# Scores of two key tiles in one stretch, value products in one stretch, turned probabilities in place

## The reference

```
x = x + cross_attention(layernorm(x), ctx)            # 16 sequences of 256 rows, 256 channels
y = layernorm(x)
for layer in range(2):                                # on y
    q, k, v = split(shift_token(y) @ wqkv)            # 8 heads of 64
    q, k = l2norm(q)*qs, l2norm(k)*ks; rotary_xpos(q, k)
    o = local_attention(q, k, v)                      # windows of 128 rows, each sees itself and the one before
    y = y + o @ wo
    h = layernorm(shift_token(y)) * lg + lb
    a, g = split(h @ w1 + b1)
    y = y + (a * gelu(g)) @ w2 + b2
x = x + y
```

## Time and profile before

| | |
|---|---|
| median of 3 runs | 1419.7 us (1419.18 to 1420.46) |
| profiled execution, span | 1416.2 us |
| what lies around the span (median less span) | 3.5 us |
| TensorE busy | 1385.3 us (98%) |
| VectorE, ScalarE, GpSimd busy | 77%, 66%, 54% |
| chain that ended last | TensorE 65%, VectorE 16%, ScalarE 9% |

### The profile page before, as it was taken

One profiled execution on the slowest core, in us unless ns is written; L12 is line 12 of the kernel. 1 busy time (PEld: TensorE's weight loads), 2 busy tenths in 40 slices (PEclk: granted clock), 3 DMA queues, 4 the chain that ended last, 5 costly groups with the idle time before them and its releaser, 6 DMA issues.

```text
span 1416.2 us, 32735 instructions
## 1 busy us (share of the span) xinstructions
PE 1385.3 (98%) x11563; PEld 1237.8 (87%) x11563; DVE 1090.6 (77%) x3067; ACT 935.8 (66%) x2662; POOL 761.9 (54%) x576
## 2 busy tenths in 40 slices
PE   8999999989999999999999999999999999999998
PEld 7999998778888888888888888888888888888887
DVE  5777776768788788888888878778778888888874
ACT  6877777456666666666666667666666666666662
POOL 1212222556566566666666667666656666666653
PEclk9999999999999999999999999999999999999999
DMA  5223122101100100010001211111111111111001
GB/s 190 90 92 110 48 67 90 47 20 29 30 30 30 30 29 28 28 28 28 28 29 29 71 29 37 33 35 37 37 37 37 36 36 36 36 36 37 29 30 31
DMA packets 50516, 63.41 MB, mean 45 GB/s; under 512 B 8402, under 2 KB 32104, under 8 KB 50408
## 3 DMA queue, kind: packets, MB, share of 16 engines
q1 hardware_dynamic: 50408, 61.99, 14.0%
HBM read 38.17 MB, written 16.78 MB: 39 GB/s over the span
## 4 chain that ended last, share of the span: by engine, by line
PE 65%; DVE 16%; ACT 9%; issue 5%; DMA 2%; POOL 1%; SPq 1%; DVEq 0%; ACTq 0%; POOLq 0%
PE pb L567 30%; PE pb L880 6%; PE pb L894 6%; PE pb L856 5%; PE pb L825 5%; PE pb L840 5%; ACT x_p L1079 4%; PE pb L920 4%; DVE p_t L1596 2%; DVE p_t L1610 2%; ACT x_pt L1085 2%; DVE r_sin L1583 2%; DVE n_sq L1562 2%; DMA x<-x 1%; DVE r_cos L1577 1%
## 5 line engine op out<-in xcount | busy, mean ns | idle before, releaser
L1823 POOL TENSOR_TENSOR n_inv<-n_cl,half_neg 128x16 f32<-128x16 f32 x64 | 211.2, 3299 | 178.2 <-DVE n_cl L1567 174.7
L1222 ACT ACTIVATE p_t<-p_t,s_nm 128x128 f32<-128x128 f32 (+1 forms) x512 | 227.0, 447 | 22.3 <-DVE s_nm L1596 20.9
L567 PE MATMUL pb<-h_hi,w_hi 128*128 128x256 f32 x704 | 207.5, 295 | 1.3 <-DVE h_lo L1558 1.2
L567 PE MATMUL pb<-h_hi,w_lo 128*128 128x256 f32 x704 | 198.7, 282 | 0.0
L567 PE MATMUL pb<-h_lo,w_hi 128*128 128x256 f32 x704 | 198.6, 282 | 0.0
L1828 POOL TENSOR_TENSOR r_cos<-r_cos,r_sin 128x1024 f32<-128x1024 f32 x64 | 154.6, 2415 | 53.8 <-DVE r_sin L1583 53.8
L1213 ACT ACTIVATE pt_t<-pb 128x512 f32<-128x512 f32 x192 | 114.3, 597 | 98.5 <-PE pb L840 97.8
L1178 ACT ACTIVATE qk_sq<-pb 128x512 f32<-128x512 f32 x128 | 72.5, 592 | 142.9 <-PE pb L567 141.5
L567 PE MATMUL pb<-wqkv_hi,xt_hi 128*128 128x512 f32 x384 | 163.9, 427 | 2.6 <-DVE r_sin L1583 2.3
L1859 POOL TENSOR_TENSOR hg_lo<-hg,hg_hi 128x256 fp32r<-128x256 f32 (+1 forms) x192 | 141.9, 760 | 44.5 <-DVE hg_hi L1627 44.5
L1596 DVE CUSTOM_DVE_ANT_0 p_t<-pb,mask_t 128x128 f32<-128x128 f32 (+1 forms) x512 | 151.9, 353 | 17.5 <-PE pb L825 17.3
(11 more groups left out here) (145 smaller groups left out, 3907.5 us busy)
## 6 DMA issues: line engine op xcount, KB each, us to landing
y_state<-x SPq DMA_DIRECT2D x32, 256.0 KB, 2.0
x_cur<-y_state SPq DMA_DIRECT2D x32, 256.0 KB, 2.6
x_res<-y_state SPq DMA_DIRECT2D x32, 256.0 KB, 2.8
x_in<-x SPq DMA_DIRECT2D x16, 256.0 KB, 2.9
x_state<-x SPq DMA_DIRECT2D x16, 256.0 KB, 2.0
x_orig<-x_state SPq DMA_DIRECT2D x16, 256.0 KB, 2.9
out<-x SPq DMA_DIRECT2D x16, 256.0 KB, 2.2
x<-x SPq DMA_DIRECT2D x32, 112.0 KB, 2.3
```

The source lines that it names most:

```text
L567: mm = pe.matmul(dst, s, m, start=(n == 0 and k == 0), stop=(n == len(pairs) - 1 and k == 2))
L1222: e = nc.scalar.activation(pu, pu, ACT.Exp, bias=s_nm[:, j, k:k + 1], scale=-1.0, accum_out=s_sum[:, j, k:k + 1])
L1823: nc.gpsimd.tensor_tensor(n_inv[:, t], n_cl[:, t], half_neg[:], ALU.pow).then_inc(pool_inv, 1)
```

## The change

The two score stretches over 256 keys run one after the other at the head of the iteration, in four different banks; the three value-product stretches become one behind T5; the copies of the turned probabilities go back into `p_t` and the tile `pt_t` is gone. TensorE's order becomes:

scores 0, scores 1, P01, P00, F0, F1, P02, F2, P10, F3, F4, scores 2, T0, P11, F5, turn_h, P12, T1, T2, turn_next, T3, H0, T4, H1, H2, T5, W0 W1 W2, H3, H4, O0, H5, Q0 to Q3, O1.

The orders of VectorE, ScalarE, GpSimd and SyncE are not changed.

```
-        pt_t = sb("pt_t", [P, 4, 512], where=L)
-        S_BANK = [3, 4, 3, 4, 3, 4]
+        S_BANK = [3, 4, 5, 6, 3, 4]
-            def scores(a, b, j):
+            def scores(a, b, c, j):
                 if j == 0:
                     ...
+                elif j == 1:
+                    if c is not None:
+                        pe.wait_ge(dve_x1, at(c, 1, 1))
                 else:
-                    pe.wait_ge(dve_max, at(b, UNITS, 2 * j))
+                    pe.wait_ge(dve_max, at(b, UNITS, 2))
             def turn_p(a, b, d, u):
                 pe.wait_ge(dve_pn, at(b, UNITS, u + 1))
+                if u == 0:
+                    pe.wait_ge(dve_max, at(b, UNITS, 3))
-            def weigh(b, c, par, j):
-                pe.wait_ge(act_pt, at(b, UNITS, 2 * j + 2))
-                if j == 0:
-                    pe.wait_ge(act_v, at(b, NT, NT))
-                    if c is not None:
-                        pe.wait_ge(dve_x1, at(c, 1, 1))
-                ... (products of units 2j and 2j+1 from pt_t)
+            def weigh(b, c, par):
+                pe.wait_ge(act_pt, at(b, UNITS, UNITS))
+                pe.wait_ge(act_v, at(b, NT, NT))
+                pe.wait_ge(dve_max, at(b, UNITS, 4))
+                for j in range(3):
+                    ... (the same products from p_t)
                 mm.then_inc(pe_av, 1)
...
                 if b is not None:
-                    scores(a, b, 0)
+                    scores(a, b, c, 0)
+                    scores(a, b, c, 1)
...
                     feed(c, d, 1)
-                if b is not None:
-                    scores(a, b, 1)
...
                 if b is not None:
-                    weigh(b, c, 1 - par, 0)
                     turn_p(a, b, d, 3)
...
                     turn_p(a, b, d, 5)
-                    weigh(b, c, 1 - par, 1)
-                    weigh(b, c, 1 - par, 2)
+                    weigh(b, c, 1 - par)
...
             def probs_copy(b, u):
                 act.wait_ge(pe_pt, at(b, UNITS, u + 1))
-                if u == 4:
-                    act.wait_ge(pe_av, at(b, 3, 1))
-                elif u in (0, 2) and later(b):
-                    act.wait_ge(pe_av, at(plus(b, -1), 3, 3 if u == 0 else 2))
-                nc.scalar.activation(pt_t[:, u % 4], pb[:, PT_BANK[u]], ACT.Copy).then_inc(act_pt, 1)
+                nc.scalar.activation(p_t[:, u], pb[:, PT_BANK[u]], ACT.Copy).then_inc(act_pt, 1)
...
             def out_hi(b):
-                act.wait_ge(pe_av, at(b, 3, 3))
+                act.wait_ge(pe_av, at(b, 1, 1))
...
                 dve.wait_ge(pe_s, at(b, UNITS, j + 1))        # in maxes(b, j)
                 if later(b):
-                    dve.wait_ge(pe_pt, at(plus(b, -1), UNITS, j + 1))
+                    dve.wait_ge(pe_av, at(plus(b, -1), 1, 1))
```

More of the change, by code:

```diff
@@ L841, in turn_p @@
                 mm.then_inc(pe_pt, 1)
-            def weigh(b, c, par, j):
-                pe.wait_ge(act_pt, at(b, UNITS, 2 * j + 2))
-                if j == 0:
-                    pe.wait_ge(act_v, at(b, NT, NT))
-                    if c is not None:
-                        pe.wait_ge(dve_x1, at(c, 1, 1))
[L850 to L858, removed]
+            def weigh(b, c, par):
[3 more added lines that the diff above has]
+                for j in range(3):
+                    for k in range(2 if j < 2 else 4):
+                        for t in range(NT if j < 2 else 1):
+                            for u in (2 * j, 2 * j + 1):
+                                h = heads_of(u)[k]
+                                r, col = (h % 2) * DH, (h // 2 % 2) * T + (P if j < 2 else 0)
+                                piece = 2 * k + t if j < 2 else k
+                                mm = pe.matmul(pb[r:r + DH, 6 + h // 4, col:col + P], v_t[:, par, t, h * DH:h * DH + DH],
+                                               p_t[:, u, piece * P:piece * P + P],
+                                               start=(t == 0), stop=(t == NT - 1 or j == 2))
                 mm.then_inc(pe_av, 1)
@@ L965, in run_l @@
                 if b is not None:
-                    scores(a, b, 2)
+                    scores(a, b, c, 2)
                     turn_p(a, b, d, 0)
```

## The result

The changed kernel takes 1487.24 us (median of 4 runs, 1486.59 to 1488.93), the kernel before 1419.44 us in the same runs. The ratio is 1.0487, 95% interval 1.0472 to 1.0502: 67.8 us slower. The forecast was slower by 45.8 us, 1465.5 us, with a range up to 1475. The direction was right and the size was not; a third of the loss was not foreseen.

A forecast was written before the change was run, and what follows sets the result against it. The prediction took the chain from F5 over VectorE and GpSimd to PN5 to set T5; -0.24, 0 and +1.65 made +1.41 us an iteration, times 32 and corrected +45.8, so 1465.5 us, range 1447 to 1475.

The forecast's parts named there:

- PN5 sets T5: F5 to T5: VectorE's division PN5, behind clamp 1 and GpSimd's add, sets T5's time; TensorE's own work merely fits in front.
- The value products, +1.65 us: T5 to H3: 16 more products in the stretch cost 0.88 us, standing for T5's copy 0.77 an iteration.
- The head, -0.24 us: Iteration head: one score stretch fewer saves 0.29 us, the new wait for the residual costs 0.05.
- Score banks, maxes ... Each 0: Scores and maxes: earlier scores bring maxes 2 and 3 nothing, and new waits are met several us earlier; each 0.
- scores in one stretch: Iteration head: merging two score stretches saves one start and end and a slower step, taken as 0.29 us.
- F5 to T5: 0: Middle of the iteration: taking W0 out buys nothing, T5 stays 9.83 us behind F5.
- +1.7 for them: Irregular iterations: in some 6, VectorE is late at the head and the 0.29 us is not saved, +1.7 us.
- A: Rival at clamp 1: clamp slips ahead of GpSimd's add, T5 0.36 us earlier, +1.05 an iteration, 1453 us; chance 0.08.
- B: Rival, F5 to T5: TensorE paces all queues, T5 comes 1.28 us earlier, 1422 us, no measurable change; chance 0.05.
- C: Rival: T5's copy 0.6 us late or the residual uncovered, +0.5 more an iteration, time 1481; chance 0.10.

The follow-up runs named there:

- e8: The kernel before, with scores 1 and scores 2 in one stretch behind F1: 1415.71 us, ratio 0.9982 to the kernel before.
- e5: The kernel before, with scores 1 and 2 merged behind F1 and GpSimd's inverse_norms of tile 1 ahead of its add_parts: 1407.17 us, ratio 0.9928.
- e2: The changed kernel, with value products back in three places, each with its own wait for copies, copies still in place: 1438.95 us, ratio 1.0142.
- e3: The changed kernel, but only the last third of the value products waits for T5's copy: 1465.68 us, ratio 1.0335.
- e1: The changed kernel, with scores 1 back behind F1 and the value products still in one stretch: 1467.97 us, ratio 1.0347.
- e10: The changed kernel, with scores 1 moved between P00 and F0: 1461.56 us, ratio 1.0305.
- e7: The changed kernel, with F3 and F4 ahead of P10 on TensorE: 1488.42 us, ratio 1.0495.
- e4: The changed kernel, with GpSimd's inverse_norms of tile 1 ahead of its add_parts of tile 1: 1477.68 us, ratio 1.0418.

## Why the prediction was right or wrong

**PN5 sets T5: right.** T5 starts 0.05 us behind PN5's end in the changed kernel as well, and e8 and e5 show that TensorE's savings are worth next to nothing without, and something with, an earlier PN5. Taking W0 out from between F5 and T5 bought nothing: in e2 it is back, and T5 stands where it stood (25.35 us).

**The value products, +1.65 us: right.** Measured 1.35 + 2.77 = 4.12 us from T5 to H3 (1151.92 to 1156.04) against 2.48 in the earlier trace rows: +1.64. Its two parts are the standing for the copy, 1.35 instead of 0.58 = 0.77, of which e3 gives 0.75 back, and the products' own 2.77 instead of 1.90 = 0.87. e1, which has this part alone, is 49.5 us slower than before.

**The head, -0.24 us: this step failed.** Its sentence "Score banks, maxes ... Each 0" and the term "scores in one stretch" priced what the moved stretch saves and what it waits for, and not what it stands in front of. Scores 1 issue 0.86 us of work ahead of P01 and P00, with a wait for the residual of some 0.15 (I took 0.05; the stretch is 2.08 us instead of 1.93). P00 comes 1.0 us later, and so do the squares and the table load; the rotation is 0.91 us late and clamp 0 is 0.89. Head to F5 costs +0.25 us instead of -0.24, and head to T5 +0.89; e2 has this part alone, and is 20.5 us slower. e10 shows that it is the late P00: with scores 1 behind P00 instead of ahead of P01, and nothing else moved, T5 is back at 24.5 us.

**F5 to T5: 0. Wrong by 0.64,** for the same reason: the chain no longer hangs on F5 (1094.13 to 1103.96 before = 9.83 us, 1141.45 to 1151.92 after = 10.47) but on P00. I took the 0.53 us of the earlier trace rows as proof that F5 was the anchor, and as room for everything else on VectorE. It was neither. Between second_residual and clamp 0 stand the inverse sums, which need ScalarE's exponentials of unit 4, and before the change these ended at 1095.03 + 0.19 = 1095.22:

```profile
1095.03 0.19 ACT L1222 ACTIVATION_READ_ACCUMULATOR p_t<-p_t,s_nm 128x1 f32 x1
1095.27 0.17 DVE L1604 RECIPROCAL s_inv<-s_sum 128x4 f32<-128x4 f32 x1
```

The second chain, rotation, maxes 4, exponentials, was at most 0.05 us behind F5's and not half a microsecond. At its start the squares ended at 1083.76 + 1.09 = 1084.85, some 0.1 us before the rotation began (1084.97). So of the 1.0 us of the late P00 0.91 reached the rotation and 0.89 clamp 0, and an earlier F5 gained next to nothing in e8. In the changed kernel e7 moves F5 alone, and T5 doesn't follow.

**The sum.** In the regular iteration +0.89 + 1.64 = +2.53, measured 37.82 - 35.30 = 2.52. Over the 31 periods it is 69.4 us, 2.24 each, as irregular iterations, which were longer before, lose less; my +1.7 for them had the wrong sign.

**The rivals.** A: no clamp slipped ahead by itself (1.60 us in both); e4 forced it, and the gain was the 0.36 us of its floor. (By the prediction's own terms this floor is 1100.61 + 24 x 0.12 = 1103.49; the missing 0.11 is H1's first product, which takes 0.23 instead of 0.12, as from 1148.56 on in the changed kernel, so 1103.60 holds.) B: T5 came 0.89 us later behind the head and not 1.28 earlier, so TensorE does not pace the queues. C came nearest in size, with another mechanism: the wait for the residual was only partly uncovered (0.15), and T5's copy was on time (1152.62, 0.70 behind T5).

## What to carry to other kernels

When an instruction stretch is moved ahead, price each thing that it now stands in front of on its own queue, and follow each of them through the other engines to the point that sets the period. A merge that saves mode changes is best put where the stretch behind it has time to spare, as behind F1 here. And where a wait of half a microsecond marks a chain's anchor, look for the next-latest input before building a sum on it, at the instructions behind the wait too: here it was some 0.05 us away, one instruction further on, and the profile shows no wait for it.

## What the runs showed of the hardware that I had not expected

GpSimd's power over 128 x 16 and a VectorE operation over 128 x 512 with both inputs in SBUF run side by side, and neither is longer for it by more than 0.03 us. In the changed kernel:

```profile
1143.58 3.31 POOL L1819 TENSOR_TENSOR n_inv<-n_cl,half_neg 128x16 f32<-128x16 f32 x1 [5.66 <-DVE n_cl L1563]
```
```profile
1144.58 0.69 DVE L1554 TENSOR_TENSOR h_lo<-h_n,h_hi 128x512 fp32r<-128x512 f32 x1
```

VectorE's operation begins 1.0 us into the power and takes 0.69 us, as in all 30 iterations where the two meet so. The power takes 3.31 us here and 3.28 at 1151.35. The same VectorE operation took 1.12 us the one time that it began inside one of GpSimd's splits of 128 x 256:

```profile
1466.69 1.12 DVE L1554 TENSOR_TENSOR h_lo<-h_n,h_hi 128x512 fp32r<-128x512 f32 x1
```

And GpSimd's add over 128 x 1024 held VectorE's 128 x 16 clamp for 1.43 us (1.60 instead of 0.17). The length of a GpSimd operation does not tell whether it blocks VectorE; which property of it does, no run here separates.

Two score stretches in one, 24 instructions, take no second start and end: the saving of 0.29 us a stretch, worked out from the rows of before, appeared as 0.32 us of F5 in e8.
